# Feed-forward stages by halves of the token positions, two of the four halves placed inside the slots of the delta stage

## The reference

```python
# feed-forward: a recurrence over the 4 batches, element by element over the token positions
f = sigmoid(x_t @ wf.T + c @ uf.T + bf);  i = sigmoid(x_t @ wi.T + c @ ui.T + bi)
g = tanh(x_t @ wc.T + c @ uc.T + bc);     c = f * c + i * g
out_t = tanh(x_t @ wo.T + c_last @ uo.T + bo)      # c_last: the state after the last batch
...
# delta: in every head, chunk after chunk of the sequence, a state S is carried on
U = solve_triangular(eye + A, vc * bc[:, None] - kb @ S, lower=True)
o = qc @ S + jnp.tril(qc @ kc.T) @ U
return (S + kc.T @ U, o)
```

## Time and profile before

| | us |
|---|---|
| three executions | 1452.35, 1454.43, 1455.84 (median 1454.43) |
| the profiled execution: its own time | 1452.64 |
| its span | 1450.8 |
| attention | 0 to 646 |
| first feed-forward stage | 646 to 831 |
| delta | 831 to 1256 |
| second feed-forward stage | 1256 to 1445, then the last store to 1451 |

### The profile page before, as it was taken

One profiled execution on the slowest core, in us unless ns is written; L12 is line 12 of the kernel. 1 busy time (PEld: TensorE's weight loads), 2 busy tenths in 40 slices (PEclk: granted clock), 3 DMA queues, 4 the chain that ended last, 5 costly groups with the idle time before them and its releaser, 6 DMA issues. The chain is left out here.

```text
span 1450.8 us, 32359 instructions
## 1 busy us (share of the span) xinstructions
PE 1218.1 (84%) x13530; PEld 755.3 (52%) x13530; DVE 880.1 (61%) x1900; ACT 610.2 (42%) x1207; POOL 447.5 (31%) x663
## 2 busy tenths in 40 slices
PE   3779999999999999989999346566987858699993
PEld 1434444444444444337888323245665647488882
DVE  4466767676788777715434755677867362354346
ACT  1426666666666766655222322122332212142222
POOL 2420505142200000014231556443663313342304
PEclk7889999999999999999999768778999979899996
DMA  5492535344455333000000000011111100000003
GB/s 153 131 148 90 89 45 89 56 78 67 73 63 62 49 45 45 2 1 1 1 0 1 17 17 10 21 32 29 33 29 32 35 25 12 2 1 0 1 1 116
DMA packets 78754, 61.66 MB, mean 43 GB/s; under 512 B 41360, under 2 KB 65552, under 8 KB 78480
## 3 DMA queue, kind: packets, MB, share of 16 engines
q1 hardware_dynamic: 77456, 57.18, 21.9%
q10 hardware_dynamic: 1152, 2.41, 0.5%
HBM read 38.20 MB, written 20.97 MB: 41 GB/s over the span
## 5 line engine op out<-in xcount | busy, mean ns | idle before, releaser
L694 ACT ACTIVATE weights<-psum 128x512 f32<-128x512 f32 (+1 forms) x608 | 322.4, 585 | 159.4 <-PE psum L607 157.5
L739 DVE TENSOR_REDUCE maxima<-psum 128x1 f32<-128x512 f32 (+3 forms) x432 | 262.2, 662 | 57.4 <-PE psum L538 56.3
L607 PE MATMUL psum<-q_stack,k_stack 99*128 99x512 bf16 (+3 forms) x768 | 223.7, 328 | 1.3 <-ACT weights L694 1.1
L538 PE MATMUL psum<-k_stack,q_stack 96*128 96x512 bf16 (+3 forms) x768 | 213.0, 328 | 5.8 <-DMA k_stack<-qk_parts 4.1
L624 PE MATMUL psum<-weights,v_rows 128*17 128x512 f32 (+3 forms) x1536 | 162.0, 494 | 0.1
L510 POOL TENSOR_TENSOR residual<-residual,att_o 128x256 f32<-128x256 f32 x32 | 23.2, 725 | 364.0 <-DVE att_o L772 364.0
L900 PE MATMUL psum<-f_xT,f_weights_hi 128*128 128x512 f32 x384 | 123.5, 403 | 0.0
L739 DVE TENSOR_REDUCE negmax<-psum 128x1 f32<-128x384 f32 (+3 forms) x176 | 102.3, 634 | 27.8 <-PE psum L538 26.2
L607 PEld LDWEIGHTS psum<-q_stack,k_stack 99*128 99x128 bf16 x768 | 72.5, 98 | 83.1 <-ACT weights L694 38.6
L965 ACT ACTIVATE f_gates<-psum,ffn_biases 128x512 f32<-128x512 f32 x72 | 49.7, 690 | 155.8 <-PE psum L906 155.8
L1335 PE MATMUL psum<-d_w_qkb,d_hT 128*128 128x260 f32 x128 | 48.0, 510 | 68.3 <-DVE d_attnT_k_kb_v L1505 57.8
(11 more groups left out here) (165 smaller groups left out, 2277.9 us busy)
## 6 DMA issues: line engine op xcount, KB each, us to landing
qk_parts<-a_parts SPq DMA_DIRECT2D x32, 384.0 KB, 3.6
q_stack<-qk_parts SPq DMA_DIRECT2D x90, 128.0 KB, 7.1
k_stack<-qk_parts SPq DMA_DIRECT2D x90, 128.0 KB, 7.8
residual<-in_x SPq DMA_DIRECT2D x8, 512.0 KB, 7.5
out_x<-residual SPq DMA_DIRECT2D x8, 512.0 KB, 3.8
ffn_weights<-in_ffn_w ACTq DMA_DIRECT2D x1, 2048.0 KB, 9.1
systems<-d_a_rows SPq DMA_DIRECT2D x32, 64.0 KB, 1.8
d_systems<-systems SPq DMA_DIRECT2D x4, 512.0 KB, 4.8
```

The lines of the kernel that those rows point to most:

```text
L538: m = e.matmul(out[:, i * width:(i + 1) * width], self.qst[st][0:self.ROWS, h, qb * P:(qb + 1) * P], self.kst[st][0:self.ROWS, h, k0:k0 + ...
L607: m = e.matmul(out[:, j * width:(j + 1) * width], self.kst[st][0:self.ROWS + self.MAX_ROWS, h, kb * P:(kb + 1) * P], self.qst[st][0:self.R ...
L694: e.activation(self.weights[n % 2][:, heads[0]:heads[-1] + 1, 0:width], bank[self.score_bank[n, i]][:, 0:len(heads) * width].rearrange("p ...
L739: e.tensor_reduce(to, bank[self.bank[item]][:, 0:len(heads) * width].rearrange("p (h x) -> p h x", h=len(heads)), AXIS_X, ALU.max, negate= ...
```

## The change: what it does

`Ffn` becomes `Feed` (the weights, split once, for both stages) and `Half` (one half of the positions, t = 0 to 3). A `Half` is a list of items, each with its piece of work on every engine: norm (layernorm statistics and scaling), turn (transpose), gate, ahead (the part of a gate that needs no state, issued before that gate's state is there), hid, cu (the output of the state), sum, join. A half's items are in this order:

```diff
+        self.start = [("norm", 0), ("turn", 0, 0), ("turn", 0, 1), ("norm", 1)]
+        self.rest = []
         for t in range(B):
+            gates = [("gate", t, mt, g) for mt in range(KT) for g in range(3)]
+            self.rest += ([("ahead", *gates[0][1:]), ("ahead", *gates[1][1:])] if t else []) + gates[:4]
+            self.rest += [("turn", t + 1, 0), ("turn", t + 1, 1)] if t + 1 < B else []
+            self.rest += ([("norm", t + 2)] if t + 2 < B else []) + gates[4:] + [("hid", t, 0), ("hid", t, 1)]
+        self.end = [("cu", 0), ("cu", 1), ("sum", 0)]
+        for t in range(1, B):
+            self.end += [("sum", t), ("join", t - 1)]
+        self.end += [("join", B - 1)]
```

`build` places the items. Each slot of the delta stage has two places for guests, one after the projections (on DVE: before the products of the chunk before), one at the slot's end (on DVE: before `solve(2 * CH)`):

```diff
+        begun = 3
+        opening, rest = first[0].start[:3], first[0].start[3:] + first[0].rest
+        last_turn = rest.index(("turn", B - 1, KT - 1)) + 1
+        alone = of(first[0], rest[:last_turn]) + of(first[1], [("norm", 0)]) + of(first[0], rest[last_turn:])
+        alone += of(first[1], first[1].start[1:] + first[1].rest[:begun]) + of(first[0], first[0].end)
+        beside = first[1].rest[begun:] + first[1].end
+        ahead = second[0].start + second[0].rest + second[0].end
...
+        left = spread(first[1], beside, range(FIRST_SLOT, LATE), lambda slot: (2, 2))
+        assert not left
+        left = spread(second[0], ahead, range(KEEP + 4 + LAG_S, LAST_SLOT), lambda slot: (1, 1 + slot % 2))
+        last = of(second[1], second[1].start[:1]) + of(second[0], left)
+        last += of(second[1], second[1].start[1:] + second[1].rest + second[1].end)
```

For room in memory, the delta stage has one buffer in place of two for its transposed input and its normed rows, the sigmoid of the convolution is written where the product goes, `gate` has 16 entries in place of 17, and the products of the solve are laid close together:

```diff
-KEEP, GATES, SUMS = 16, 17, 24
+KEEP, SUMS, LATE = 16, 24, 9
...
-                e.activation(self.sig[:, :], self.acc[:, :], ACT.Sigmoid).then_inc(*s["sigm"].did(G, kt))
+                for w in unmet(s["conv"](G, kt, TAPS - 1), s["vg_mm"]((G - 2) * TPG + TPG - 1) if G >= 2 else None):
+                    e.wait_ge(*w)
+                e.activation(self.hT[G % 2][:, kt, :, :, :].rearrange("p c b t -> p b c t"),
+                             self.acc[:, :].rearrange("p (b c t) -> p b c t", b=B, c=TPG), ACT.Sigmoid).then_inc(*s["sigm"].did(G, kt))
...
-            e.tensor_tensor(self.prod[:, 0:done, 0:left], row, below, ALU.mult).then_inc(*s["inv_mul"].did(n, i))
+            e.tensor_tensor(products, row, below, ALU.mult).then_inc(*s["inv_mul"].did(n, i))
```

More of the change, by code:

```diff
@@ L1606, in vector @@
                 solve(4)
+            for half, item in self.visit(slot, 1):
+                half.vector(e, unmet, item)
             if phase == 5:
@@ L1622, in sync @@
+        first[0].place(first[0].end, [2, 3, 4], [2, 3, 4], held)
+        first[1].place(beside, [5, 6, 7], [5, 6, 7], held)
+        held = {}
+        second[0].place(ahead, [2, 3], [2, 3], held)
+        second[1].place(second[1].start + second[1].rest + second[1].end, [4, 5, 6, 7, 2, 3], [0, 1], held)
         def sync(e, unmet):
```

672 lines of the change are left out of this document (353 added, 319 removed).

## The result

The changed kernel takes 1479.26 us (median of 4, 1475.02 to 1484.64) against 1454.07 for the kernel before in the same session: a ratio of 1.0175, interval 1.0136 to 1.0214. The forecast was 1443, at most 1466. It is 25 us slower.

What follows compares the result with a forecast made beforehand. PE was taken as full in the feed-forward stages, with room in delta slots. Net -13.9 us for the first stage and +3.9 from slot 36 on gave -10.0, a span of 1440.8; forecast 1443, range 1415 to 1466.

Steps and rivals of the forecast that it cites:

- the state's chain of a lone half: First stage's lone first half: chain of about 5.3 us hidden behind 5.64 us of matmuls, costing 1 us over three times.
- the lower clock behind waits: PE's first gates at lower clock: 1.5 us in the first stage's lone half, 1.7 us after the delta stage.
- the walk through slots -5 to 8: Queue walk with guests: slots -5 to 0 take 43 us for 24.7, slots 1 to 8 take 95.8 for 55.7.
- 8.4 us of layernorms: Up to the first keys: two layernorms on POOL, delta's and guest's, stand ahead of a gate product the next state needs.
- rival 2: Slots 1 to 8: guests' state chains on DVE keep it from the keys; 125 us there, 1472 in all; chance 0.18.
- the ring's wait: Slots 1 to 8: PE idles 2.77 us a slot until ACT, DVE, POOL and DVE's keys allow the next projection.
- The price of half a stage in matmuls at full clock: Feed-forward stages: one half costs PE 72.8 us in all, and 2.8 for the output of the state.
- the gap between the halves: Second feed-forward stage: a PE gap of 13 to 15 us between its halves, named as a sign of being right.
- Rival 1: Slots -5 to 8: PE becomes the bound, guests' DVE work falls into gaps; 1414 us; chance 0.20.
- rival 4: Second stage: waits around the solve, in slots 39 to 51 and of state chains cost 15 us less; 1428; chance 0.15.
- the head of 15.0 us: Second feed-forward stage's start, not PE's: claimed gone after the change, with no bias and no splits there.
- Rival 3: The lock: half of POOL's 32 gate products hold a DVE instruction on the path, 19 us; 1462; chance 0.10.

Runs made afterwards that it cites:

- e4: The change with each half's layernorm for batch t + 2 moved behind the gates and hidden products of batch t; 1473.7 us, ratio 1.013 to the kernel before.
- e16: The change with ACT's scaling of the output weights moved from the head of the delta stage to slot 9; 1474.5 us, ratio 1.014 to the kernel before.
- e5: The change with DVE doing a slot's second guests only after the next chunk's keys, in slots up to 8; 1478.9 us, ratio 1.016 to the kernel before.
- e1: The change without guests (feed-forward items inside delta slots): all four halves one after another, each stage as a whole; 1514.0 us, ratio 1.040 to the kernel before.
- e9: e8 with the pieces in the order of the kernel before, such as a block's layernorm one step ahead; 1450.5 us, ratio 0.999 to the kernel before.
- e12: e9 with the second stage's t = 0 of the first half as guests in slots 39 to 51; 1459.3 us, ratio 1.004 to the kernel before.
- e8: The change without guests, both stages' halves alternating, each half with its own buffer for normed rows; 1487.0 us, ratio 1.022 to the kernel before.
- e17: The change with e4, e5, e16 and the second half's first gates ahead of the first half's end in the second stage; 1453.1 us, ratio 0.999 to the kernel before.
- e15: e9 with the first stage's ten end pieces as guests in slots -4 to 0, last state on DVE behind the delta's first statistics; 1442.5 us, ratio 0.992.
- e13: e1 with e9's order in each lone half: layernorm one block ahead, transposes between the hidden products; 1548.5 us, ratio 1.065 to the kernel before.

## Why the prediction was wrong

The forecast was a small win and the change loses 25 us. Three steps of the sum failed: the state's chain of a lone half, put at 1 us; the lower clock behind waits, put at 1.5 and 1.7 us; and the walk through slots -5 to 8, which let guests run in time that engines spend waiting in order.

**The lone halves were mis-sized: +12.4 of the first 14.5 us, and the larger part of the last 10.4.** The step reads "hidden to within 0.3 us, three times: 1 us", and the same 1.2 us for the second stage's last half. It is true of the chain by itself: in e4 1.4 us of waits for the state are left. But I wrote the chain without the layernorm that stands ahead of its gate product in POOL's queue. I had counted that in slots -5 to 0, and not here. Measured are 4.91, 1.30 and 1.43 us of waits in the first half, 4.89 and 1.22 in the last, and behind the two long ones 12 and some 9 matmuls at half pace. e4 takes 8.5 us out of F1 and 7.7 out of F2, and makes slots 32 on 4.0 longer. All waits of PE up to the output of the state are 12.7 us where the sum has 8.4, and three stretches at half pace cost 7.4 where it has 1.5: 10.2 of the 12.4, the rest is not accounted for. The other 2.1 of the 14.5 are a first gate at 657.9 where 655.8 was forecast.

**Slots -5 to 0: +11.3.** "8.4 us of layernorms" was not the longest wait. A wait of ACT for a transfer, 7.68 us long and harmless before, got guests behind it. The walk through these slots names POOL's and DVE's work and no wait of ACT, which is busy 5.0 of 24.7 us; but idle time of an engine can be a wait, and then it is not room. e16 shows 8.5 of the 11.3.

**Slots 1 to 8: +11.1.** The mean of a slot is 13.4 us, the very point from which rival 2 was to decide. From keys to keys the eight slots took 15.0, 20.5, 9.9, 13.0, 17.9, 12.0, 10.3 and 8.2 us; the second and the fifth, 4.7 and 4.3 above the forecast, make most of the miss. Rival 2 had its place right (slot 2: the state ahead of the keys) and its mechanism only in part: e5 takes the guests away from in front of the keys and wins 3.3 us. Its 1472 lies near the measured time by luck: it had 125 us for these slots, and they took 106.9. The step that failed is the one that let guests of PE run inside the ring's wait. PE's busy time came out as forecast and its idle time did not shrink but grew by 5.4 us, in e5 by 4.7. In the kernel before, all of PE's waits there, some 20 us, end with the keys; in the change 17.6 still do, and 6.2 more are the guests' own: 1.75 for ACT (840.41), 1.41 and 3.02 for DVE (850.19, 901.33). What made the fifth slot long was not separated further.

**The clock was costed at 1.5 and 1.7 us.** In e1 it makes some 13.9 us of one stage. In the first half of the change three stretches of 5.3 us run at 0.50 (rows in the last section), where the sum has one, of 1.5 us; it has nothing behind the waits for the state and for the low parts.

**What was right.** The price of half a stage in matmuls at full clock, nearly the gap between the halves (12.2 us, forecast 13 to 15), slots 36 to 38 with the solve, slots 39 to 51, nothing lost in slots 9 to 35 to the smaller buffers (e9 shows the same with no guests). Against lone halves without guests (e1) the guests of the second stage win 13.1 us and those of the first 17.3; against alternating halves the second stage's lose (e12, 8.9 us). Rival 1 had no part, rival 4 at most 2.6 us. That the head of 15.0 us goes because bias and splits go is not borne out: e9 has neither at that place and the same head; the change has no head because its first half is done by then. Rival 3, the lock of DVE and POOL, is seen: the product of 512 columns on POOL takes 1.77 us beside DVE's product (857.65) and 1.26 alone (678.00). The Trainium skill (SBUF — State Buffer, section "SBUF: two separate sides") describes such a lock. By that rule, the trace agrees. Of the 32 products of that kind on POOL in the changed kernel 24 took 1.57 to 1.81 us and 8 took 1.26 to 1.29, which is 12 us in all if every one of them were waited for, an estimate from these rows; six of DVE's products in the kernel before already lost 1.0 us each. What the lock costs by itself no run shows.

**The frame.** The sum set "PE has room there" against "PE is full here". The runs say: two alternating halves in the right order (e9) hide their chains behind each other for nothing, and the sequence of halves of the change pays 60 us (e1) before a guest has won anything; alternation alone, in the change's order, gives 27 of them back (e8). With 35 won, the change ends 25 behind; with the waits repaired (e17) it comes to the kernel before; and with the halves left alternating and only the stage's tail as guests (e15) it is 11 us ahead of it.

## What to carry to other kernels

Before work is moved into another stage's idle time, write down for every engine, also the idle ones, what it waits for there: a wait that nobody stood behind becomes a wait of the guests, and of the stage's own work that is queued behind them. What the move breaks up (here two halves that covered each other) is a cost to be run alone, without any guest, before the overlap is judged. Of a piece that several engines share, check its place in the queue of each, since the same order of pieces that made alternating halves whole (e9) made lone ones 34 us slower (e13 against e1).

## What was not expected of the hardware

The granted clock is the part that was least expected. Nearly the same matmuls (x794 before, x800 in e1) took 153.9 us of PE at a mean granted clock of 0.94 and 167.8 at 0.90. After the wait of 4.91 us, the two sixes up to 687.52, which take 1.40 us each at full clock, took 2.7 and 2.6; after the one of 5.05 us, projections took 2.10 and 3.62 us instead of 1.14 and 1.88. The halving is that between 2.4 and 1.2 GHz. So a wait of 5 us of PE cost some 7.5 us at both places. The stretches behind the start of the stage and behind the waits of 4.91, 3.75 and 5.05 us, in the columns of the earlier trace rows:

```profile
657.90:663.16 5.26, 5.26 (x13) 4.10 (x13) 5.26 (x11) 4.66 (x8) 0.00 (x0) 0.50 0.00 0
682.24:687.52 5.28, 5.28 (x12) 4.13 (x13) 0.55 (x1) 0.69 (x1) 0.00 (x0) 0.50 0.00 0
750.76:756.02 5.26, 5.26 (x13) 4.10 (x13) 1.45 (x8) 0.69 (x1) 3.53 (x7) 0.50 0.00 0
863.32:868.60 5.28, 5.28 (x9) 2.86 (x9) 2.54 (x10) 0.62 (x3) 2.88 (x6) 0.50 0.00 0
```

PE is busy all the time in each of them, at a granted clock of 0.50. Behind the waits of 1.30 and 1.43 us the clock did not fall: it is 1.00 from 706.83 to 729.00 and from 729.04 to 745.00.
